# A network of eight sublayers on one core: the first and third feed-forward blocks each in one block of code, the tile loop with held weights, and two ternary weights quantised later

## The reference

```python
# L0_ffn: 2 shared experts, 16 routed, the 4 likeliest of them used
up_s = jnp.einsum('th,seh->tse', xt, shared_up)
shared = jnp.einsum('tse,she->th', jax.nn.gelu(up_s, approximate=False), shared_down)
probs = jax.nn.softmax(xt @ router_w.T, axis=-1)
topk_p, topk_i = jax.lax.top_k(probs, TOP_K)
gate = jnp.zeros_like(probs).at[jnp.arange(xt.shape[0])[:, None], topk_i].add(topk_p)
up_r = jnp.einsum('th,reh->tre', xt, routed_up)
act = jax.nn.gelu(up_r, approximate=False) * gate[:, :, None]
routed = jnp.einsum('tre,rhe->th', act, routed_down)
...
# L2_ffn: V = x Wv, 8 experts of inner width 32, top 2 by two scores r and c
s = _ln(r, g_r, b_r) + jax.nn.sigmoid(alpha) * _ln(c, g_c, b_c)
topv, sel = jax.lax.top_k(s, K)
...
# L3_ffn: 8 experts 256 -> 1024 -> 256, top 2
topk_logits, topk_idx = jax.lax.top_k(logits, K)
gates = jax.nn.softmax(topk_logits, axis=1)
h = jax.nn.relu(jnp.einsum('td,edh->teh', xf, W1) + b1)
y = jnp.einsum('teh,eho->teo', h, W2) + b2
```

## Time and profile before

| | before |
|---|---|
| time, median of 3 runs | 1756.88 us |
| its runs | 1756.88, 1757.24, 1754.15 us |
| the profiled execution | 1757.79 us |
| its span | 1756.0 us |
| mean granted clock of TensorE | 0.919 |
| busy: PE | 1458.9 us (83%) |
| busy: DVE | 998.6 us (57%) |
| busy: ACT | 798.9 us (45%) |
| busy: POOL | 581.9 us (33%) |
| l0_ffn | 75.5 to 331.4 us |
| l2_ffn | 1033.7 to 1144.4 us |
| routed_tiles, within l3_both | 1423.9 to 1756.0 us |

### The profile page before, as it was taken

The page is one execution under the profiler, slowest core; times in us unless marked ns, Lnnn a source line. Parts: engine busy times, 40 slices in busy tenths (PEclk is TensorE's granted clock), DMA queues, the critical chain, the costliest instruction groups (busy, mean ns, idle before and its releaser), DMA issues. The chain is left out here.

```text
span 1756.0 us, 28182 instructions
## 1 busy us (share of the span) xinstructions
PE 1458.9 (83%) x8616; PEld 1085.2 (62%) x8630; DVE 998.6 (57%) x2448; ACT 798.9 (45%) x1905; POOL 581.9 (33%) x784
## 2 busy tenths in 40 slices
PE   4669999599999999586999968744757559999997
PEld 3458888577777777354777745521534436666765
DVE  3668888855555555487566646355765423333332
ACT  2444444465555555286655533244647213233231
POOL 0068887454434333301545300000102522222222
PEclk9869999799999999898999999866987669999999
DMA  7000004149100000100000000050002721111110
GB/s 267 1 25 24 24 24 155 40 139 284 46 1 1 1 1 1 37 1 4 1 1 1 1 24 1 1 195 0 1 1 97 265 75 50 48 48 47 51 43 7
DMA packets 63737, 89.34 MB, mean 51 GB/s; under 512 B 7024, under 2 KB 55040, under 8 KB 62720
## 3 DMA queue, kind: packets, MB, share of 16 engines
q1 hardware_dynamic: 58336, 75.08, 13.9%
q0 software_dynamic: 5280, 12.74, 2.2%
HBM read 56.09 MB, written 33.54 MB: 51 GB/s over the span
## 5 line engine op out<-in xcount | busy, mean ns | idle before, releaser
L1264 POOL TENSOR_SCALAR XT<-XT,l1x_rs 128x256 f32<-128x256 f32 x256 | 118.4, 483 | 189.3 <-DVE l1x_rs L1176 189.3
L1121 ACT ACTIVATE XT<-bank,l1x_nmax 128x256 f32<-128x256 f32 x256 | 118.7, 471 | 68.6 <-DVE l1x_nmax L1180 68.6
L1180 DVE TENSOR_REDUCE l1x_nmax<-bank 128x2 f32<-128x512 f32 x128 | 87.5, 685 | 109.6 <-PE bank L1028 109.6
L2342 PE MATMUL bank<-l3x_wu,XT 128*128 x312 | 142.6, 600 | 0.8 <-issue 0.8
L2351 PE MATMUL bank<-l3x_wd,CT 128*128 x624 | 141.5, 380 | 1.8 <-DVE CT L2419 1.8
L1040 PE MATMUL bank<-ident,XT 128*128 128x128 f32 x768 | 120.6, 279 | 8.9 <-POOL XT L1264 3.3
L2351 PEld LDWEIGHTS bank<-l3x_wd,CT 128*128 128x128 f32 x624 | 115.6, 190 | 17.1 <-issue 2.9
L837 DVE SCALAR_TENSOR_TENSOR X<-bank,l0f_gates,X 128x256 f32<-128x256 f32 x288 | 118.8, 473 | 0.0
L1040 PEld LDWEIGHTS bank<-ident,XT 128*128 128x128 f32 x768 | 84.0, 140 | 42.7 <-POOL XT L1264 24.0
L2386 ACT ACTIVATE CT<-bank,l3x_b 128x128 f32<-128x128 f32 x156 | 44.5, 368 | 139.7 <-PE bank L2360 139.7
L1187 DVE COPY l1x_pt<-bank 128x512 f32<-128x512 f32 x128 | 87.9, 687 | 29.7 <-PE bank L1040 29.7
(11 more groups left out here) (518 smaller groups left out, 3902.6 us busy)
## 6 DMA issues: line engine op xcount, KB each, us to landing
slots<-blank SPq DMA_DIRECT2D x9, 1987.5 KB, 22.8
l3x_wu<-in_L_ffn_W SPq DMA_DIRECT2D x8, 1024.0 KB
l3x_wd<-in_L_ffn_W SPq DMA_DIRECT2D x8, 1024.0 KB
XT<-slots SPq DMA_DIRECT2D x39, 132.5 KB, 2.1
l0e_wu<-in_L_ffn_upT SPq DMA_DIRECT2D x18, 128.0 KB, 2.1
l0e_wd<-in_L_ffn_downT SPq DMA_DIRECT2D x18, 128.0 KB, 2.3
X<-in_x SPq DMA_DIRECT2D x1, 2048.0 KB, 8.7
tern_back<-in_L_xattn_W_f1T SPq DMA_DIRECT2D x1, 2048.0 KB, 10.4
```

The costliest lines, as they stand in the source:

```text
L1121: act.activation(pr[n % 3][:, i, q, :], sc[(2 * n + i) % 3][:, q * S:(q + 1) * S], ACT.Exp, bias=nmax[:, n % 3, i, q:q + 1], accum_out=sum ...
L1180: dve.tensor_reduce(nmax[:, n % 3, i, :], sc[(2 * n + i) % 3][:].rearrange("p (q s) -> p q s", q=QT), AX, ALU.max, negate=True).then_inc(m ...
L1264: pool.tensor_scalar(t, t, rs[:, n % 3, i, q:q + 1], 1.0, ALU.mult, ALU.mult).then_inc(norm_ok, 1)
L2342: last = pe.matmul(up_b[half][:], xT[:, k, :], wu[:, ds(e * KD + k, 1), half * CH:(half + 1) * CH].rearrange("p a n -> p (a n)"), start=k ...
```

## The change

It has four parts.

1. **l0_ffn in one block.** The functions `layernorm`, `router` and `small_experts` are replaced by one block without a loop on the device. TensorE turns chunk after chunk (`turn_rows`) and starts the units of the first experts, whose gate is 1, between them. The router's products come after unit 2's `hidden`, now with the router's 16 columns held and 512 rows moving (L637: 2 products a chunk), ScalarE copies their result out, and TensorE turns it in 16 small products. VectorE computes probabilities, choice and gates between the additions of units 4 to 7. ScalarE writes `XT` and `XH` both from the banks; GpSimd computes `XL` chunk by chunk after splitting expert 0's weights.
2. **l2_ffn in one block.** Layernorm is woven with the first products. The scores, the choice and Silu are done for halves of 8 tiles instead of chunks of 4. `vT` and the hidden values are kept for all chunks. The wide products go through two banks, the outputs through two others. ScalarE makes both copies of the turned hidden values.
3. **routed_tiles with held weights.** `up` now holds a 128 × 128 block of the first weights and moves the 128 turned rows: 16 products of 128 columns give the hidden values already turned. `turn_hidden` and the copies L2380 and L2411 are gone. The chosen expert's first weights are copied two tiles ahead to one of two fixed places (`chosen`), one half by ScalarE, the other by VectorE (128 × 1024 elements each). `xT`, `hT` and the result banks are doubled.
4. **Ternary weights.** All ten are still loaded and summed in `l0_cosine`. GpSimd quantises eight of them (8 pieces) in `l0_ffn`, two steps an expert; the other two (6 pieces, 3 MB) are loaded again in `l2_ffn`, quantised there by GpSimd, which had nothing to do in that stage, and stored at its end. The thresholds are computed once, at the end of `l0_cosine`.

The diff, cut to its core:

```diff
 # l0_ffn, TensorE
+                turn_rows(0)
+                turn_rows(1)
+                hidden(0)
+                turn_rows(2)
+                hidden(1)
+                outputs(0)
+                turn_rows(3)
+                hidden(2)
+                outputs(1)
+                route(0)
+                route(1)
+                hidden(3)
+                outputs(2)
+                route(2)
+                route(3)
+                hidden(4)
+                outputs(3)
+                turn_logits()
+                for n in range(4, N):
+                    if n + 1 < N:
+                        hidden(n + 1)
+                    outputs(n)
...
 # l0_ffn, GpSimd
+                split(0)
+                for c in range(NC):
+                    low_rows(c)
+                    if c == 1:
+                        split(1)
+                for e in range(2, E):
+                    split(e)
+                    for n in range(done, min(done + 2, ternary.steps())):
+                        ternary.step(pool, n)
+                    done += 2
...
 # l2_ffn, VectorE
+                normalise(0)
+                normalise(1)
+                normalise(2)
+                dve.wait_ge(loaded, LOADED)
+                add_bias(0)
+                normalise(3)
+                add_bias(1)
+                choose(0)
+                add_bias(2)
+                weigh(0)
+                add_bias(3)
+                choose(1)
+                weigh(1)
+                for c in range(NC):
+                    add_outputs(c)
...
 # l2_ffn, TensorE
+                turn_rows(0)
+                turn_rows(1)
+                pe.wait_ge(loaded, LOADED)
+                first_products(0)
+                turn_rows(2)
+                first_products(1)
+                turn_rows(3)
+                first_products(2)
+                first_products(3)
+                turn_hidden(0)
+                for c in range(NC):
+                    outputs(c, 0)
+                    if c + 1 < NC:
+                        turn_hidden(c + 1)
+                    outputs(c, 1)
...
 # routed_tiles, TensorE
                 def up(i):
-                    e = expert(pe, i)
                     pe.wait_ge(xT_ok, i + 1)
+                    pe.wait_ge(w_act, i + 1)
+                    pe.wait_ge(w_dve, i + 1)
                     for half in range(2):
-                        for k in range(KD):
-                            last = pe.matmul(up_b[half][:], xT[:, k, :], wu[:, ds(e * KD + k, 1), half * CH:(half + 1) * CH].rearrange("p a n -> p (a n)"),
-                                             start=k == 0, stop=k == KD - 1)
+                        if i >= 2:
+                            pe.wait_ge(hT_act if half == 0 else hT_dve, i - 1)
+                        for j in range(HT // 2):
+                            m = half * (HT // 2) + j
+                            for k in range(KD):
+                                last = pe.matmul(up_b[i % 2][half][:, j * P:(j + 1) * P],
+                                                 chosen[i % 2][:, k, m * P:(m + 1) * P], xT[i % 2][:, k, :],
+                                                 start=k == 0, stop=k == KD - 1)
                         last.then_inc(up_done, 1)
...
 # routed_tiles, VectorE
+                def choose(i):
+                    e = expert(dve, i)
+                    if i >= 2:
+                        dve.wait_ge(up_done, 2 * (i - 1))
+                    dve.tensor_copy(chosen[i % 2][:, 1, :], wu[:, ds(e * KD + 1, 1), :].rearrange("p a n -> p (a n)")).then_inc(w_dve, 1)
...
+                    last_one.then_inc(hT_dve, 1)
+                    if i + 2 < SLOT_TILES:
+                        choose(i + 2)
                     if i:
                         output(i - 1)
```

More of the change, by code:

```diff
@@ L389, in done, with pieces @@
+    def pieces(self):
+        return self.columns // self.PIECE
     def done(self, pieces):
@@ L707, in small_experts, with l0_ffn @@
-def small_experts(K, name, E, XH, XL, up, down, gates, ternary):
-    nc, X, bank = K.nc, K.X, K.bank
+@stage
+def l0_ffn(K):
+    nc, a, X, XT, bank, ternary = K.nc, K.a, K.X, K.XT, K.bank, K.ternary
+    NS, ER, TOP = 2, 16, 4
+    E = NS + ER
+    N = E * NC
+    W = ER + 8 - TOP
     YB = bank[4:8]
```

807 lines of the change are left out of this document (403 added, 404 removed).

## The result

The changed kernel takes 1729.3 us (median of 4, 1724.9 to 1732.0) against 1756.7 for the kernel before: a ratio of 0.984, with a 95% interval of 0.982 to 0.987, or 27 us less. The forecast was 1723, with a range of 1710 to 1736.

A forecast was written before the change was run, and what follows sets the result against it. TensorE was taken to pace l0_ffn after a serial head, l2_ffn to be partly serial, and TensorE and GpSimd's chain nearly equal in the loop; −16 − 12 − 6 + 0 = −34 gave 1723 us, range 1710 to 1736.

The forecast's parts named there:

- the rival of 1863: Tile loop: weight loads of up's 32 rows not hidden, a tile 11.5 us, the whole 1863 us; chance 0.05.
- The loop's term: Tile loop: TensorE's period falls to 7.3, GpSimd's unchanged chain of 7.58 a tile sets the pace; −6 us (−15 to +3).
- 9.4 for long links: Tile loop: about 6 scatter-to-gather links lengthened where instruction fetches meet a scatter, 9.4 us in all.
- the rival of 1749: Tile loop: GpSimd's scatter issue waits for VectorE's new copy, up to 0.69 us a tile, the whole 1749; chance 0.15.
- −16 forecast: l0_ffn: parts summed to 240 us against 255.9, routing no longer ahead of the products; range −10 to −22.
- two result banks cover about one unit, so I charge 5: l0_ffn: allowance of 5 us for TensorE stalls from VectorE's routing work between units.
- −12 forecast: l2_ffn: waits between chunks and the separate layernorm go, stage ends after 97 to 99 us; range −3 to −18.
- the ternary weights' 0: l2_ffn and l0_cosine: moved quantisation and sums are covered by other work, cost 0; +6 if cover is gone.
- a GpSimd comparison doesn't hold VectorE: l0_ffn trace, applied to l2_ffn: L830 took its usual 0.69 us inside comparison L441; only a TENSOR_TENSOR locks VectorE.
- by the row for 6 × 2.6 = 16 at most, mostly where VectorE waits anyway: l2_ffn: six moved quantisation pieces block VectorE at most 16 us, against up to some 50 by the skill page.
- the walk through the lists: l2_ffn: new instruction lists followed engine by engine with the stage's durations, giving an end after 97 to 99 us.
- The rival of 1735: l2_ffn gains nothing: serial VectorE chains, locked by GpSimd's TENSOR_TENSORs, replace the removed waits; the whole 1735; chance 0.12.

The follow-up runs named there:

- chain_free: Changed kernel with the tile loop's scatter sent to three scratch arrays, gathers not waiting for the previous scatter, accumulation left out; loop 272.7 us.
- changed_again: The changed kernel unaltered, run again beside a later group; ratio to the kernel before 0.987 (0.983 to 0.990), loop 294.1 us.
- loop_only: The kernel before with the changed routed_tiles alone; 1731.3 us beside 1748.9 for the kernel before, loop 287.4 us.
- merged_whole: Changed kernel, both shared experts' results summed in TensorE's banks, choice in one piece behind unit 6; ratio to the kernel before 0.981, 1716.9 us.
- shared_merged: Changed kernel, both shared experts' results summed in TensorE's banks, l0_ffn's choice in four pieces; ratio to the kernel before 0.984, l0_ffn 245.8 us.
- l2_no_quant: Changed kernel without GpSimd's quantisation of the last two ternary weights in l2_ffn, zeros written instead; l2_ffn 97.8 us for 105.8.
- merged_front_late: Changed kernel with merged shared experts, one-piece choice, all ten ternary weights quantised in l0_ffn from expert 4; ratio to the kernel before 0.983.

## Why the prediction was right, and where its terms were off

**The forecast's mechanism for the loop held.** TensorE's period fell to 7.24 (forecast 7.3) with weight loads hidden, and the rival of 1863 is out. By the Trainium skill, "TensorE: Matmul & The Clock Gate", section "The mechanism", where it says that a load overlaps a running product only if their row groups differ, that rival would have come; 32 loads of full row groups in 3.57 us, beside their products, speak against it. GpSimd's chain, unchanged in each link, became the pace in every tile, which chain_free shows by taking it away.

The loop's term was −6 and measured −11.0; from first to last sum the forecast had 297.4 us and the trace has 291.6. What was mis-sized are first the tiles at the end. Tiles 33 and 35 to 38 move next to nothing, and their chain is 6.5 us long, as from gather to gather here:

```profile
1704.40 1.04 POOL L2356 DMA_INDIRECT XT<-out_x,XT  x1 [1.91 <-DMA out_x<-XT]
...
1710.90 1.04 POOL L2356 DMA_INDIRECT XT<-out_x,XT  x1 [1.94 <-DMA out_x<-XT]
...
DMA packets 96, 0.00 MB, mean 0 GB/s; under 512 B 96, under 2 KB 96, under 8 KB 96
```

96 packets and 0.00 MB in 6 us. Before, TensorE's 7.98 hid that. The trace showed it all the same, in the last gather, 2.3 us ahead of the last sum of the earlier trace rows, where I had read 3.04 as fixed:

```profile
1743.15 1.04 POOL L2325 DMA_INDIRECT XT<-out_x,XT  x1 [1.96 <-DMA out_x<-XT]
```

The six periods from tile 32 on are 5.2 us shorter than six of 7.58. The 32 periods ahead of them are 8.7 us longer than 32 of 7.58, where I had put 9.4 for long links. That this came out so near is luck, since the number of long links changes from run to run: 6 in the changed kernel, 8 in changed_again, 3 in loop_only, with loops of 291.6, 294.1 and 287.4. Of the 11.0 us, 4.6 were gained in the first 19 periods, in which the chain set the pace before too, by fewer and shorter long links. Here is the longest of the changed kernel, tile 21's:

```profile
1593.32 1.00 POOL L2358 DMA_INDIRECT out_x<-XT  x1 [3.37 <-DVE XT L2451]
1598.26 1.04 POOL L2356 DMA_INDIRECT XT<-out_x,XT  x1 [3.94 <-DMA out_x<-XT]
...
q8 instruction: 1, 0.02, 1.1%
```

4.94 from scatter to gather, and one packet of an instruction fetch within it. In four traces (the kernel before, the changed one, changed_again, loop_only) 77 of the links from scatter to gather behind the first have a packet of q8 or q14 in their window, and 20 of these are over 3.9 us; of the 71 without a packet none is over 3.3. So a packet always stands beside a long link, but most packets lengthen nothing, and no run took the fetches away: the cause is likely and not shown.

**VectorE's copy in the loop** didn't lengthen the chain: the rival of 1749 is out. The scatter still comes 0.79 to 0.85 after the sum in every tile. The Trainium skill, "SBUF — State Buffer", section "SBUF: two separate sides", has such a copy keep GpSimd from writing descriptors. Here it starts 0.8 us or more after GpSimd's last issue began, and an issue takes 1.0, so this trace doesn't refute the rule; it shows only that this order is harmless.

**l0_ffn: −16 forecast, −9.3 measured.** Head 8.5 (8.8 forecast) and tail 4.7 (5.4) were right. Between them the sum had 216.1 us of products and twice 5 for stalls, 226.1, and the trace has 233.4. The step that failed is "two result banks cover about one unit, so I charge 5": TensorE waited 9.1 us for VectorE between 84 and 133, 6.15 of it once, and 11.1 in the stage, and the pause cost 2.1 more through the clock, of which the sum had nothing at that place. The rest, about 4 us, are products that ran longer elsewhere, some 3 of it at the lower clock ahead of 97 us. Why 5 was too little: a unit leaves VectorE 0.5 us, so hardly anything of the routing is taken up by slack, whether it comes in one piece or four. The waits fell only in merged_whole, where additions went and the choice stood in the room they had left; with additions gone alone (shared_merged) they stayed at 10.6. At −9.3 the term is just outside its own range of −10 to −22.

**l2_ffn: −12 forecast, −4.9 measured, and the ternary weights' 0.** These two belong together. The step that failed is "a GpSimd comparison doesn't hold VectorE", read from one pair of rows (L441 and L830), and with it "by the row for 6 × 2.6 = 16 at most, mostly where VectorE waits anyway". l2_no_quant gives 97.8 us without the work, within my 97 to 99; with it 105.8. So the walk through the lists was right, and the 8.0 us are the price of the quantisation in that stage, which I had at 0. VectorE's operations beside comparisons took 8.0 us more of its own time, those that met a TENSOR_TENSOR, the only ones I had counted, 3.0; and VectorE had no room for it, since the two choices lie on TensorE's path.

The rule of the Trainium skill in "SBUF — State Buffer", section "SBUF: two separate sides", has GpSimd and VectorE lock each other out for a whole instruction, where VectorE's has two SBUF inputs and GpSimd's reads SBUF, or where VectorE's runs in a 2-port mode. The comparisons read SBUF, so the rule was nearer than my reading. But the trace agrees only in part: under one and the same L339, L1678 took 0.88 us more and L1679, with two inputs as well, its usual 0.29; in l0_ffn L757 ran at 0.69 and the gates took 1.22 for 0.42. What decides it no run here shows, nor whether L1677, with its one input, ran in such a mode. I had weighed the page against a single instance, and chosen the instance.

Sum: −9.3 − 4.9 − 11.0 and −0.5 elsewhere give −25.7; the forecast had −34, with two terms too large by 7 each and one too small by 5. That the total lies within the range is in part luck, since the loop's error took off a third of the other two. The rival of 1735 ("l2_ffn gains nothing") is no farther from the measured 1729.3 than the forecast is, and half of its mechanism came true: GpSimd's operations did lock the serial chains, though l2_ffn still gained 4.9 us.

## What to carry to other kernels

Before work is moved beside a serial stretch of an engine, compare the engine's slack per unit with the work: if a unit leaves 0.5 us, cutting the piece smaller changes nothing; work taken away helps, and only if the piece then stands where the room is. An idle engine isn't free when its work lengthens that of the engine that sets the pace: price work on GpSimd by running the stage without it, not by one pair of overlapping rows, and look where its result is stored: a store issued late can end the stage (4.8 us in merged_front_late). And where two chains of almost equal length run side by side, shorten the one until the other shows, then read the other's links in every kind of tile, the empty ones too.
